# Moving the products of the old state with the decayed queries to another visit and another bank

## The reference, cut to what matters

```
def step(S, inp):
    A_i, v_i, wk_i, rkg_i, wkg_i, intra_i = inp
    v_corr = A_i @ v_i
    wk_corr = A_i @ wk_i
    v_new = v_corr - wk_corr @ S
    o_i = rkg_i @ S + intra_i @ v_new
    S = gamma_C * S + wkg_i @ v_new
    return (S, o_i)
...
h = silu(lin(x, w1) * ...) * lin(x, w2)
h = gelu(lin(h, h1)); h = gelu(lin(h, h2)); out = lin(h, w3)
```

## Time and profile before

| | |
|---|---|
| median of 3 runs | 1715.2 us (1713.33 to 1718.22) |
| the profiled execution, its own time | 1712.34 us |
| its span, first to last instruction | 1710.5 us |
| PE busy | 1679.5 us, 98% of the span |
| DVE, ACT, POOL busy | 65%, 57%, 35% |
| mean granted clock of PE | 0.989 of full |
| DMA, mean rate | 54 GB/s |

### The profile page before, as it was taken

One profiled execution on the slowest core, in us unless ns is written; L12 is line 12 of the kernel. 1 busy time (PEld: TensorE's weight loads), 2 busy tenths in 40 slices (PEclk: granted clock), 3 DMA queues, 4 the chain that ended last, 5 costly groups with the idle time before them and its releaser, 6 DMA issues.

```text
span 1710.5 us, 60827 instructions
## 1 busy us (share of the span) xinstructions
PE 1679.5 (98%) x25144; PEld 1613.7 (94%) x25144; DVE 1118.3 (65%) x3167; ACT 974.2 (57%) x2277; POOL 595.9 (35%) x694
## 2 busy tenths in 40 slices
PE   8799999999999999999999999999999999999999
PEld 5598999999999999999999999999999999999998
DVE  5677667667667666667666666766666666676432
ACT  4564555555655555655555665556665555665554
POOL 3544232433332433332343333343333243433111
PEclk8799999999999999999999999999999999999999
DMA  8202223322223222223222223222223332222100
GB/s 283 83 15 39 49 54 57 55 42 51 47 53 61 52 42 52 45 54 61 52 49 48 45 51 60 55 52 42 52 49 56 54 58 42 49 49 48 20 15 13
DMA packets 396496, 92.21 MB, mean 54 GB/s; under 512 B 368372, under 2 KB 388472, under 8 KB 396216
## 3 DMA queue, kind: packets, MB, share of 16 engines
q1 hardware_dynamic: 394224, 85.87, 25.6%
q10 hardware_dynamic: 1992, 2.38, 0.5%
HBM read 45.07 MB, written 30.94 MB: 44 GB/s over the span
## 4 chain that ended last, share of the span: by engine, by line
PE 92%; DVE 1%; ACT 1%; POOL 1%; issue 1%; DMA 0%; SPq 0%; ACTq 0%; DVEq 0%
PE mlp L1214 65%; PE mlp L1288 7%; PE solo L1214 3%; PE duo L1502 3%; PE solo L1371 3%; PE solo L1187 1%; PE duo L1423 1%; PE duo L1491 1%; PE duo L1180 1%; PE duo L1396 1%; PE duo L1175 1%; PE solo L1197 1%; PE duo L1493 1%; PE duo L1383 1%; POOL act_lo L697 1%
## 5 line engine op out<-in xcount | busy, mean ns | idle before, releaser
L1214 PE MATMUL mlp<-act_hi,w_hi 128*128 128x256 f32 x4096 | 970.7, 283 | 2.7 <-POOL act_lo L697 1.5
L1214 PE MATMUL mlp<-act_lo,w_hi 128*128 128x256 f32 x4096 | 949.6, 278 | 0.0
L1214 PEld LDWEIGHTS mlp<-act_hi,w_hi 128*128 128x128 f32 x4096 | 771.3, 188 | 13.2 <-issue 1.7
L1214 PEld LDWEIGHTS mlp<-act_lo,w_hi 128*128 128x128 f32 x4096 | 771.7, 188 | 1.4 <-issue 0.6
L843 ACT ACTIVATE full<-mlp,scale_sb 128x256 f32<-128x256 f32 x512 | 243.4, 475 | 528.1 <-PE mlp L1214 527.9
L933 DVE TENSOR_TENSOR act_lo<-full,act_hi 128x256 fp32r<-128x256 f32 x512 | 251.8, 492 | 313.6 <-ACT act_hi L844 312.2
L697 POOL TENSOR_TENSOR act_lo<-full,act_hi 128x256 fp32r<-128x256 f32 x256 | 186.8, 736 | 485.1 <-ACT act_hi L833 485.1
L844 ACT ACTIVATE act_hi<-mlp,scale_sb 128x256 fp32r<-128x256 f32 x512 | 240.5, 470 | 0.3 <-issue 0.3
L1214 PE MATMUL mlp<-xh,w_hi 128*128 128x256 f32 x768 | 182.7, 280 | 3.3 <-issue 3.3
L1214 PE MATMUL mlp<-xl,w_hi 128*128 128x256 f32 x768 | 181.8, 279 | 0.0
L1065 DVE SCALAR_TENSOR_TENSOR full<-mlp,scale_sb,gate 128x256 f32<-128x256 f32 x192 | 92.9, 484 | 90.8 <-ACT gate L828 88.3
(11 more groups left out here) (184 smaller groups left out, 2634.9 us busy)
## 6 DMA issues: line engine op xcount, KB each, us to landing
w_raw<-in_wts SPq DMA_DIRECT2D x22, 512.0 KB, 5.2
kg<-r SPq DMA_DIRECT2D x64, 126.0 KB
xin<-in_x SPq DMA_DIRECT2D x62, 128.0 KB, 2.8
out_y<-y SPq DMA_DIRECT2D x62, 128.0 KB, 2.5
x_squares<-o_state SPq DMA_DIRECT2D x30, 256.0 KB, 3.2
vn<-x_squares SPq DMA_DIRECT2D x120, 64.0 KB, 2.2
h_squares<-near SPq DMA_DIRECT2D x28, 256.0 KB, 4.3
hT<-h_squares SPq DMA_DIRECT2D x112, 64.0 KB, 2.4
```

The source lines that it names most:

```text
L1214: mm = pe.matmul(dst, *general_ops, start=is_first and i == 0, stop=is_last and i == 1)
```

## The change

In the steps of the list `mixed`, `old_state` leaves the lead and becomes a group of its own in the long visit, between `pred` and `gram`. It writes to `solo1` in place of `duo1`. ACT copies it to `o_state` behind `l3` column 3 in place of `l2` column 0, and before that waits for `x_out`, since `o_state` must have been moved out. In the lead, PE waits for that copy (`o_state_ready`) in place of `rg_ready`, and `own` stands alone. Steps 1 and 2 keep the old way.

```diff
-        ("l3", 1): [("values", 0, 1), ("pred", 0, 0), ("gram", 0, 1), ("intra", 0, 1), ("u", 0, 0), ("fs", 0, 1)],
+        ("l3", 1): [("values", 0, 1), ("pred", 0, 0), ("old", 1, 0), ("gram", 0, 1), ("intra", 0, 1), ("u", 0, 0), ("fs", 0, 1)],
...
-        ("l3", 3): [("fs", 2, 1)],
+        ("l3", 3): [("old", 0, 0), ("fs", 2, 1)],
...
-        ("l2", 0): [("old", 0, 0), ("norm", 0, 2), ("flip", 0, 2)],
+        ("l2", 0): [("norm", 0, 2), ("flip", 0, 2)],
...
-                    if name == "old":
+                    if name == "old" and k == 0:
                         act.wait_ge(inter_full, a)
-                        act.copy(o_state[:].rearrange("p (b q) n -> p b (q n)", b=NB), duo[1][:, :, NP * DH:2 * NP * DH]).then_inc(o_state_ready, 1)
+                        if items is mixed:
+                            act.wait_ge(x_out, 16 * n - 32)
+                            act.copy(o_state[:].rearrange("p q n -> p (q n)"), solo[1][:]).then_inc(o_state_ready, 1)
+                        else:
...
-            def old_state(b, hp, c, e):
+            def old_state(b, hp, c, e, in_solo=False):
...
+                bank = solo[1][:, b * NP * DH:(b + 1) * NP * DH] if in_solo else duo[1][:, b, NP * DH:2 * NP * DH]
+                return pe.matmul(bank[half(1 - e), col:col + C], state[half(e), q, c, :], rg[half(e), q, c, :], start=True, stop=True)
...
+                    if name == "old" and k == 1:
+                        pe.wait_ge(const_in, 16)
+                        pe.wait_ge(rg_ready, a)
+                        for b, hp in pair_of:
+                            for c in range(2):
+                                for e in range(2):
+                                    mm = old_state(b, hp, c, e, True)
+                        mm.then_inc(inter_full, 1)
...
-                        pe.wait_ge(o_state_ready, a)
...
-                            pe.wait_ge(rg_ready, a)
+                            if items is mixed:
+                                pe.wait_ge(o_state_ready, a)
+                            else:
+                                pe.wait_ge(rg_ready, a)
                             pe.wait_ge(u_ready, a)
...
-                            for e in range(2) if items is not alone else ():
+                            for e in range(2) if items in (second, third) else ():
                                 last_old = old_state(b, hp, chain, e)
```

More of the change, by code:

```diff
@@ L802, in part @@
                         act.activation(mi[:].rearrange("p k n -> p (k n)"), duo[0][:, 1, 2 * NP * HB:4 * NP * HB], ACT.Copy, scale=-1.0).then_inc(mi_ready, 1)
-                    if name == "old":
+                    if name == "old" and k == 0:
                         act.wait_ge(inter_full, a)
-                        act.copy(o_state[:].rearrange("p (b q) n -> p b (q n)", b=NB), duo[1][:, :, NP * DH:2 * NP * DH]).then_inc(o_state_ready, 1)
+                        if items is mixed:
+                            act.wait_ge(x_out, 16 * n - 32)
+                            act.copy(o_state[:].rearrange("p q n -> p (q n)"), solo[1][:]).then_inc(o_state_ready, 1)
+                        else:
+                            act.copy(o_state[:].rearrange("p (b q) n -> p b (q n)", b=NB), duo[1][:, :, NP * DH:2 * NP * DH]).then_inc(o_state_ready, 1)
                     if name == "join" or name == "solve" and k == 1:
@@ L1188, in own @@
                                  v[p][half(c), b, hd * DH:(hd + 1) * DH], start=m == 0, stop=m == 2 * NP - 1)
-            def old_state(b, hp, c, e):
-                q, col = b * (H // 2) + hp, NP * DH + (2 * hp + c) * C
-                return pe.matmul(duo[1][half(1 - e), b, col:col + C], state[half(e), q, c, :], rg[half(e), q, c, :], start=True, stop=True)
+            def old_state(b, hp, c, e, in_solo=False):
+                q, col = b * (H // 2) + hp, (2 * hp + c) * C
+                bank = solo[1][:, b * NP * DH:(b + 1) * NP * DH] if in_solo else duo[1][:, b, NP * DH:2 * NP * DH]
+                return pe.matmul(bank[half(1 - e), col:col + C], state[half(e), q, c, :], rg[half(e), q, c, :], start=True, stop=True)
             def corner(m, e, q, c):
@@ L1472, in part @@
                                 last_first = first_term(m, c, 1 - c)
-                        if items is not alone:
+                        if items in (second, third):
                             last_old.then_inc(inter_full, 1)
```

## The result

The changed kernel takes 1736.09 us (median of 4 runs, 1734.4 to 1738.85) against 1715.59 us before (1713.33 to 1718.22). The ratio is 1.0125, with a 95% interval of 1.0112 to 1.0139. It is 20.5 us slower; 26 were forecast. (The kernel before has one run more here than above, so its median is 1715.59 and not 1715.2.) The two profiled executions differ by 22.1 us in their spans (1732.6 and 1710.5 us).

What follows compares the result with a forecast made beforehand. PE's own busy time was taken as the bound, with few waits. Added 0.93 less saved 0.02 us a step, over 29 steps, is 26.4 us; with the median of 1715.2 us that gives 1741 us, range 1732 to 1749.

Steps and rivals of the forecast that it cites:

- What bounds the kernel: Whole kernel: PE is busy 98% of the span; its steady-step waits total 7.2 us, and added PE time counts in full.
- A group on two quarters costs as much as 32 products on four: PE's small products: a quarter takes a record each 58 ns, so 16 products on two quarters cost as much as 32.
- Added: 0.93 us: Long visit, between `pred` and `gram`: the 16 old products as their own group on two quarters add 0.93 us a step.
- Saved in the lead: 0.02 us: Lead: `own` alone takes 0.96 us in place of 0.98 with the old products, saving 0.02 us a step.
- The waits, the copy and the bank cost nothing: `rg` is ready early, `solo1` is free, and ACT's 0.58 us copy fits in 0.97 us of idle time: no cost.
- The sum, 26.4 us: Whole kernel: a net 0.91 us a step over the 29 changed steps makes it 26.4 us slower.
- The range of the forecast case, 1736 to 1746: Total time of the case with chance 0.85: 0.85 to 1.0 us a step net, about 2 us for the runs.
- the wider range: Total time of 1732 to 1749 us, taking in part of the dearer case and a smaller addition of 0.6 us a step.
- Dearer through an emptying at each side: Rival, chance 0.07: PE empties around the new group and ACT may be late, another 0.15 to 0.4 us a step, 1746 to 1753.
- The move is free: Rival, chance 0.05: record issue sets the pace; lead loses 0.49 us, long visit gains 0.49 to 0.52; 1714 to 1716 us.
- faster: Rival, chance 0.03: `own` alone goes at record pace and `old_state` slips in beside `pred` and `gram`; at most 14 us gained.

Runs made afterwards that it cites:

- apart in the lead: Kernel before, with the 16 old products kept in the lead but placed behind the 16 of `own` instead of between them: 1737.78 us, ratio 1.0122.
- filled lead: Changed kernel plus 16 products with unused results between those of `own` in the lead, on the two quarters `own` leaves free: 1740.8 us, ratio 1.0141.
- four quarters: Changed kernel with the group of old products spread over all four quarters of the array, output no longer the reference's: 1728.22 us, ratio 1.0066.
- the run with one product: Changed kernel with only one of the 16 old products left in the long visit, copy and waits kept: 1712.55 us, ratio 0.9985.
- The runs with `join`: Kernel before with the old products moved from the lead into `join`, two beside each group (1791.87 us), or as one group behind it (1738.7 us).
- the run with the old products behind `join`: Kernel before with the old products moved out of the lead, as one group of 16 behind all of `join`: 1738.7 us, ratio 1.0152.

## Why the prediction was right

- *What bounds the kernel.* Right: PE without waits, and more time for PE goes into the total in full.
- *A group on two quarters costs as much as 32 products on four.* Right, and shown three ways: apart in the lead (0.75 us a step more without the move, as `inner` covers the rest), filled lead (16 products for 0.014 us), four quarters (0.47 us for the same 16).
- *Added: 0.93 us.* Measured 0.935. *Saved in the lead: 0.02 us.* Measured 0.013 in a steady lead.
- *The waits, the copy and the bank cost nothing.* Right by the page's waits, by ACT's rows and by the run with one product.
- *The sum, 26.4 us, against 20.5.* The step that was too simple is the lead: "What is left is `own` alone, for which I take 0.96 us", in place of 0.98. I took one steady lead for all 28. Seven were longer by 5.0 us together, with 128 records at the densest place of the step; in the changed kernel, with 96 records, none was. A row had named a part of them ("issue", 2.2 us), and I bounded all waits together by 7.2 us without asking whether the change would take one away. The mean of the 28 leads before (2.18 us) in place of one timeline would have given 26.4 - 5.0 = 21.4 us. That this comes so near to 20.5 is partly luck, as the start and the layers cancel.
- *The range of the forecast case, 1736 to 1746.* Its terms, 0.85 to 1.0 us a step and 2 us for the runs, give 1738 to 1746; the measured 1736.09 lies below that, since the stalls were left out, and inside the wider range.
- *Dearer through an emptying at each side.* Did not happen (0.935 us); the group stands between others of its own block size. The runs with `join` show an added 0.13 to 0.19 us where the block size changes.
- *The move is free; faster.* Both needed the pace of records, and the filled lead and the four quarters exclude it.

What stays open is the cause of the stalls. They look like PE running short of instructions: in the profile PE waits for nothing there. They go with the place in the code. They also go with the density of records. In the six runs with 128 or 130 records in some 2 us, 45 of 168 leads stall, 3.4 to 6.4 us in a run. Of 28 leads with 128 records in 2.75 us one does, by 0.32 us. Of 140 leads with 96 records in 1.985 us one does, by 0.36 us, in the run with the old products behind `join`. Instruction transfers of 16 KB go with them too. In the kernel before, 11 of the 28 leads had one begin in the 0.55 us ahead of them; seven of these stalled, and of the other 17 none. In all six dense runs, 42 of the 45 stalled leads had one. It is not enough by itself: the changed kernel has one that near ahead of 12 leads, and none stalls. (The run with one product has none that near, so that it has no stalls says nothing.) This is a strong correlation, and no run changed the supply by itself.

## What to carry to other kernels

Before small products are moved or regrouped, ask which quarters of the array each of them uses, and time the group that stays as well as the one that goes: work between others on idle quarters was free, and the same work as a group of its own cost 0.75 to 1.08 us a step in the three places tried, against 0.94 us of its quarters' time. Blocks of another size could not use the idle quarters in the one place where it was tried. Take the mean over all repetitions of a place, not one timeline, since rare stalls at a dense place can go away with the work that is moved; and hold a difference of 10 us of 1700 against the pace of the unchanged layer columns before giving it to the edit.

## What the runs showed of the hardware that I had not expected

- The same stream of 128x256 matmuls runs at 113.3 or at 117.7 ns at the same granted clock of 1.00, settled at its start and mostly kept to its end. The starts of the stretches, sorted by their remainder after division by 3.33333 ns (a period found by searching), fall apart. A third of the circle, chosen for each kernel, holds 44 of 52 stretches at 117.7 ns and 8 of 124 at 113.3 of the kernel before, and 42 of 51 and 12 of 128 of the changed one. In eight of the twelve profiles the same period separates best among those from 3.30 to 3.37 ns; in the other four another one does, and this one is weaker. It would explain why tiny edits elsewhere in PE's program change the pace. No run set the start on purpose, so it is not shown as a cause.
- One product of 64x64 on a quarter that is the busiest costs 0.117 us; sixteen on idle quarters cost 0.014 us together.
- Starts on PE are not in program order across quarters: `gram` began 0.16 us before the last records of the group ahead of it (801.30 against 801.46).
- A change between 32x32 and 64x64 blocks cost 0.13 to 0.19 us, though the blocks lay on different quarters.
- Small products can stall with no wait in the profile: by 0.2 to 1.3 us in 45 of 168 leads of 128 or 130 records that otherwise take 2.0 to 2.1 us, and in 1 of 140 leads with 96.
